# A windowed attention pipeline on one core: another order of its steps on four engines, and norms in pairs

## What is computed

```python
for i in range(DEPTH):                      # DEPTH 6, HEADS 16, DIM_HEAD 64, WINDOW 32
    x = attn_layer(shift_tokens(x), ...) + x
    x = ffn_layer(shift_tokens(x), ...) + x
...
q, k, v = split(x @ Wqkv)                   # per head
q = l2norm(q) * qs; k = l2norm(k) * ksc
q = q * cos * scale + rotate_half(q) * sin * scale
k = k * cos / scale + rotate_half(k) * sin / scale
# each window of 32 queries looks at its own 32 keys and the 32 before
sim  = einsum('bhwie,bhwje->bhwij', bq, bk2) * 8, masked
out  = einsum('bhwij,bhwje->bhwie', softmax(sim), bv2)
return concat_heads(out) @ Wo
```

## Time and profile before

| what | us |
|---|---|
| median of 3 runs | 2237.3 |
| lowest, highest | 2233.07, 2239.87 |
| the profiled execution | 2229.49 |
| its span, first to last instruction | 2227.6 |

### The profile page before, as it was taken

How to read it: one execution, slowest core, us unless ns; L and a number is a source line. 1 busy time by engine, 2 the same in 40 slices (tenths; PEclk the granted TensorE clock), 3 DMA queues, 4 the chain that set the end, 5 groups by cost and what they waited for, 6 DMA issues and landing times. The chain is left out here.

```text
span 2227.6 us, 82947 instructions
## 1 busy us (share of the span) xinstructions
PE 2062.4 (93%) x32996; PEld 1476.9 (66%) x32996; DVE 1627.3 (73%) x3071; ACT 1472.3 (66%) x4549; POOL 1238.2 (56%) x1377
## 2 busy tenths in 40 slices
PE   7788888999899999999998999999999989999997
PEld 3232335985776976876867859768768678587672
DVE  1598986985876966867857759668678577596673
ACT  4532326976775967867767759668678667596682
POOL 1465865764753754854647537548546465365450
PEclk9888989999999999999999999999999999999999
DMA  1321202111121211211111212112211111121010
GB/s 59 133 72 60 75 29 79 41 40 33 42 74 30 50 36 33 65 56 37 40 34 37 79 27 50 35 36 55 64 37 42 34 35 42 28 50 28 24 31 19
DMA packets 148094, 104.31 MB, mean 47 GB/s; under 512 B 15778, under 2 KB 140256, under 8 KB 146176
## 3 DMA queue, kind: packets, MB, share of 16 engines
q1 hardware_dynamic: 147712, 99.07, 16.0%
HBM read 48.31 MB, written 1.18 MB: 22 GB/s over the span
## 5 line engine op out<-in xcount | busy, mean ns | idle before, releaser
L1133 ACT ACTIVATE PR<-ps,MN 128x64 f32<-128x64 f32 x1536 | 356.6, 315 | 391.3 <-DVE MN L1255 391.1
L1383 POOL TENSOR_TENSOR QK<-PC,PS 128x256 f32<-128x256 f32 x384 | 278.9, 726 | 601.0 <-DVE PS L1294 584.1
L1388 POOL TENSOR_TENSOR QK<-QK,RN 128x512 f32<-128x512 f32 x384 | 401.6, 1046 | 158.0 <-ACT RN L1123 130.5
L1002 PE MATMUL ps<-W,XS 128*128 128x256 f32 x1536 | 396.5, 381 | 4.6 <-PEq L64 4.1
L973 PE MATMUL ps<-V,PT 64*32 64x65 f32 x12288 | 301.0, 219 | 1.2
L1002 PEld LDWEIGHTS ps<-W,XS 128*128 128x128 f32 x1536 | 262.7, 191 | 25.6 <-issue 4.9
L1384 POOL TENSOR_TENSOR QK<-PC,PS 128x256 f32<-128x256 f32 x384 | 279.1, 727 | 0.0
L988 PE MATMUL ps<-ident,QK 128*128 128x128 f32 x1536 | 252.0, 287 | 29.3 <-POOL QK L1388 29.3
L973 PEld LDWEIGHTS ps<-V,PT 64*32 64x32 f32 x12288 | 257.6, 105 | 11.3 <-ACT PT L1174 5.9
L1255 DVE TENSOR_REDUCE MN<-ps 128x4 f32<-128x256 f32 x384 | 161.6, 421 | 141.7 <-PE ps L953 135.7
L1278 DVE TENSOR_REDUCE SS<-SQ 128x8 f32<-128x512 f32 x384 | 259.3, 675 | 4.4 <-ACT SQ L1165 4.4
(11 more groups left out here) (138 smaller groups left out, 3439.5 us busy)
## 6 DMA issues: line engine op xcount, KB each, us to landing
V<-V SPq DMA_DIRECT2D x384, 97.5 KB, 2.3
scr<-B_rows SPq DMA_DIRECT2D x32, 512.0 KB, 3.5
V<-V SPq DMA_DIRECT2D x288, 32.5 KB, 2.2
W<-in_Wqkv SPq DMA_DIRECT2D x40, 192.0 KB, 2.8
TC<-in_tcos SPq DMA_DIRECT2D x6, 1024.0 KB, 5.3
TS<-in_tsin SPq DMA_DIRECT2D x6, 1024.0 KB, 8.5
WO<-in_Wo SPq DMA_DIRECT2D x6, 512.0 KB, 4.3
W<-in_W SPq DMA_DIRECT2D x6, 341.0 KB, 3.5
```

The costliest lines, as they stand in the source:

```text
L1002: mm = nc.tensor.matmul(ps[:, par, k * 2 * P:(k + 1) * 2 * P], cols[k], W[:, i, 0:2, :].rearrange("p t m -> p (t m)"), start=True, stop=True)
L1133: e = nc.scalar.activation(PR[:, m % 2, h, slot * DH:(slot + 1) * DH], ps[:, 4 + h, slot * DH:(slot + 1) * DH], ACT.Exp, scale=-1.0, bias= ...
L1383: nc.gpsimd.tensor_tensor(QK[:, par, :, 0:hd], PC[:, par, :, 0:hd], PS[:, par, :, hd:DH], ALU.add)
L1388: nc.gpsimd.tensor_tensor(QK[:, par, :, :], QK[:, par, :, :], bcast_last(RN[:, par, :], DH), ALU.mult).then_inc(qk, 1)
```

## The change

Seven things change, all in `transformer_block` but the joining of the tables:

- q's and k's transposes are called ahead of the scores, and their step is n-4 instead of n-3.
- The 16 scores and 16 values come in another order. Before, the scores ran through one head's windows, then the other's, and the values of both halves of rows went to bank 6 through four of the eight tiles. Now `spread_tiles` runs through all eight tiles in turn, in both, and the values of the two row halves go to banks 5 and 6. The scores and the transposed output move to banks 3 and 4, v's projection to bank 5, p to bank 6.
- Waits that were left to others are written out. The output's transposes, the masks and p's transposes wait for themselves.
- Log and root of the norms are taken for two steps at once on 16 columns, in odd rounds, in `norm_pair`; the clamp follows in even rounds as a `tensor_scalar` with a constant.
- ScalarE's order is new: q and k, norms, exponentials, squares, output, p, v. VectorE's order is new: the rotary products stand ahead of the sums of squares, and these are of step n, no longer n-1.
- GpSimd's rotation is of step n-2 instead of n-1.
- The tables lie in one tensor TCS, and one VectorE instruction of 1024 elements makes both products.

The diff, cut to its core:

```diff
+        spread_tiles = [(0, 0), (1, 2), (0, 1), (1, 3), (0, 2), (1, 0), (0, 3), (1, 1)]
...
             def out_transposed(n):
...
-                if n >= NSTEPS:
-                    wait(pe, pr, min(n - 5, NSTEPS))
-                    wait(pe, oT, m)
+                wait(pe, pr, min(n - 5, NSTEPS))
+                wait(pe, oT, m)
                 pe.wait_ge(on, m + 1)
...
-                for h in range(2):
-                    for j in range(8):
-                        slot, quad = slot_quad(j)
-                        c0 = PAD + s * STEP + j * WIN
-                        mm = nc.tensor.matmul(ps[32 * quad:32 * quad + 32, 4 + h, slot * DH:(slot + 1) * DH],
+                pe.wait_ge(qkT, m + 1)
+                for slot in range(2):
+                    for h, quad in spread_tiles:
+                        c0 = PAD + s * STEP + window(slot, quad) * WIN
+                        mm = nc.tensor.matmul(ps[32 * quad:32 * quad + 32, 3 + h, slot * DH:(slot + 1) * DH],
...
                 for h in range(2):
-                    for j in (0, 2, 1, 3, 4, 6, 5, 7):
-                        slot, quad = slot_quad(j)
+                    for slot, quad in spread_tiles:
+                        j = window(slot, quad)
...
-                        mm = nc.tensor.matmul(ps[32 * q:32 * q + 32, 6, g * (DH + 1):(g + 1) * (DH + 1)],
+                        mm = nc.tensor.matmul(ps[32 * quad:32 * quad + 32, 5 + slot, h * (DH + 1):(h + 1) * (DH + 1)],
...
                 wait(pe, v_cp, n)
+                wait(pe, on, n - 6)
                 for k in range(2):
-                    if k == 1:
-                        wait(pe, pr, n - 4)
...
+            def norm_pair(n):
+                p = (n - 3) // 2
+                if n % 2 == 0 or not 0 <= p < NSTEPS // 2:
+                    return
+                act.wait_ge(ssm, p + 1)
+                nc.scalar.activation(SS[:, p % 2, :], SS[:, p % 2, :], ACT.Ln, scale=LN_SCALE).then_inc(lns, 1)
+                act.wait_ge(lns, p + 1)
+                wait(act, qk, 2 * p - 2)
+                nc.scalar.activation(RN[:, p % 2, :], SS[:, p % 2, :], ACT.Exp, scale=-0.5, bias=lnb[:]).then_inc(rn, 1)
...
-                root(n)
+                copy_qk(n)
+                norm_pair(n)
                 exponents(n)
+                if u == U_FFN and t >= 0:
+                    load_set(nc, act, GELU)
+                squares(n)
                 copy_out(n)
-                if u == U_FFN and t >= 0:
-                    logs(n)
-                    load_set(nc, act, GELU)
-                copy_qk(n)
-                squares(n)
                 copy_p(n)
                 copy_v(n)
...
+                both = TCS[l % 2][:, :, 2 * s:2 * s + 2, :].rearrange("p t k c -> p t (k c)")
+                nc.vector.tensor_tensor(PCS[:, par, :, :, :].rearrange("p t a d -> p t (a d)"),
+                                        ps[:, par, :].unsqueeze(1).to_broadcast([P, 2, CH]), both, ALU.mult).then_inc(prods, 1)
...
                 least(n)
                 normalise(n)
+                tables(n)
                 norms(n)
-                tables(n)
+                clamp_pair(n)
```

More of the change, by code:

```diff
@@ L71, in mamba_block @@
         XT, XRES, XS, MOD, ident, ones, epsc = (keep[k] for k in ("XT", "XRES", "XS", "MOD", "ident", "ones", "epsc"))
-        W, QKS, QK4, TC, TS, MASKB, identb = (keep[k] for k in ("W", "QKS", "QK4", "TC", "TS", "MASKB", "identb"))
+        W, QKS, QK4, TCS, MASKB, identb = (keep[k] for k in ("W", "QKS", "QK4", "TCS", "MASKB", "identb"))
         ps = keep["ps"]
@@ L815, in transformer_block @@
         stored = [sem("stored%d" % c) for c in range(NCH)]
-        s_vz, s_ones, s_v0, s_lnb, s_least = (
-            sem(k) for k in ("s_vz", "s_ones", "s_v0", "s_lnb", "s_least"))
+        s_vz, s_ones, s_v0, s_lnb = (
+            sem(k) for k in ("s_vz", "s_ones", "s_v0", "s_lnb"))
         qkv_dram = d["Wqkv"].rearrange("l p (t i m) -> l p i t m", t=3, i=PAIRS)
@@ L913, in _, with window @@
             sp.wait_ge(w_2, 32 * DEPTH)
-        def slot_quad(j):
-            return (j % 4) // 2, (j // 4) * 2 + j % 2
+        def window(slot, quad):
+            return quad // 2 * 4 + slot * 2 + quad % 2
+        spread_tiles = [(0, 0), (1, 2), (0, 1), (1, 3), (0, 2), (1, 0), (0, 3), (1, 1)]
         @block.tensor
@@ L939, in scores @@
                     pe.wait_ge(s_ones, 2)
-                if n >= NSTEPS:
-                    wait(pe, pr, m)
-                    wait(pe, oT, m - 3)
+                wait(pe, pr, m)
+                wait(pe, oT, m - 3)
                 for h in range(2):
-                    if h == 0:
-                        wait(pe, qkT, min(n - 3, NSTEPS))
-                    if h == 1 and n >= 7:
-                        pe.wait_ge(v_sh[(n - 7) % 4], 32 * ((n - 7) // 4 + 1))
-                    nc.tensor.matmul(ps[:, 4 + h, 0:P], identb[:], MASKB[:, int(s == 0), h, :], start=True, stop=True)
-                for h in range(2):
-                    for j in range(8):
-                        slot, quad = slot_quad(j)
-                        c0 = PAD + s * STEP + j * WIN
-                        mm = nc.tensor.matmul(ps[32 * quad:32 * quad + 32, 4 + h, slot * DH:(slot + 1) * DH],
+                    nc.tensor.matmul(ps[:, 3 + h, 0:P], identb[:], MASKB[:, int(s == 0), h, :], start=True, stop=True)
+                pe.wait_ge(qkT, m + 1)
[3 more added lines that the diff above has]
+                        mm = nc.tensor.matmul(ps[32 * quad:32 * quad + 32, 3 + h, slot * DH:(slot + 1) * DH],
                                               QKT[DH * h:DH * h + DH, 0, c0:c0 + WIN],
@@ L978, in qk_transposed @@
             def qk_transposed(n):
-                m = n - 3
+                m = n - 4
                 if not 0 <= m < NSTEPS:
                     return
+                wait(pe, qkT, m)
                 pe.wait_ge(qk, m + 1)
-                if n < 5:
-                    wait(pe, qkT, m)
                 for x in range(2):
@@ L1005, in project @@
                 wait(pe, v_cp, n)
+                wait(pe, on, n - 6)
                 for k in range(2):
-                    if k == 1:
-                        wait(pe, pr, n - 4)
-                    mm = nc.tensor.matmul(ps[:, 3, k * P:(k + 1) * P], cols[k], W[:, i, 2, :], start=True, stop=True)
+                    mm = nc.tensor.matmul(ps[:, 5, (2 + k) * P:(3 + k) * P], cols[k], W[:, i, 2, :], start=True, stop=True)
                 mm.then_inc(v_ps, 1)
@@ L1015, in p_transposed @@
                     return
-                if n >= NSTEPS:
-                    pe.wait_ge(pr, m + 1)
-                    wait(pe, v_cp, NSTEPS)
-                if n < 8:
-                    wait(pe, pT, m)
+                wait(pe, pT, m)
+                wait(pe, on, m)
+                pe.wait_ge(pr, m + 1)
                 for h in range(2):
-                    if h == 1 and n < NSTEPS:
-                        wait(pe, oT, n - 7)
-                    mm = nc.tensor.transpose(ps[:, 3, (2 + h) * P:(3 + h) * P], PR[:, m % 2, h, :], ident[:])
+                    mm = nc.tensor.transpose(ps[:, 6, (2 + h) * P:(3 + h) * P], PR[:, m % 2, h, :], ident[:])
                 mm.then_inc(pT_ps, 1)
@@ L1181, in copy_v @@
                     act.wait_ge(s_ones, 2)
-                wait(act, pT_ps, n - 5)
                 wait(act, o_ps, n - 7)
@@ L1370, in scale_tables @@
                 pool.wait_ge(w_tab[l % 2], 32 * ((l + 1) // 2))
-                for tab in (TC, TS):
-                    piece = tab[l % 2][:, 2 * j:2 * j + 2, :]
+                for tab in range(2):
+                    piece = TCS[l % 2][:, tab, 2 * j:2 * j + 2, :]
                     nc.gpsimd.tensor_tensor(piece, piece, QK4[:].rearrange("p x h d -> p (x h d)").unsqueeze(1)
```

103 lines of the change are left out of this document (41 added, 62 removed).

## The result

| | before | after |
|---|---|---|
| median us (4 runs each) | 2235.72 | 2318.73 |
| lowest, highest | 2233.07, 2239.87 | 2314.26, 2320.05 |
| span of the profiled execution | 2227.6 | 2317.8 |

The changed kernel takes 1.0366 times as long, with a 95% interval of 1.0343 to 1.0389. The forecast was 2298 us, +2.7%, in a range of 2258 to 2370. The time went the way that was forecast and lies in the range; the loss was a third larger than forecast.

A forecast was written before the change was run, and what follows sets the result against it. TensorE's own stream bounds an ordinary step before, at 3.45 us; after, loops through the output's copy. +70 us for 235 ordinary steps and -9 for 11 phases' longer steps give +61: 2298 us, range 2258 to 2370.

The forecast's parts named there:

- The loop over the output's copy: ScalarE copies the output behind squares that wait for the projection; TensorE's next output transposes wait for it: +70 us.
- Loop A: From projection through squares, output's copy, transposes and tiles to the next projection: 3.72 us, 3.78 with a second restart.
- loop B: From the scores through minimum, exponentials, squares, output's copy and transposes to the next scores: 3.71 us.
- The size of an ordinary step: An ordinary step takes 3.75 us instead of 3.45, 0.30 more in each of 235 steps: +70 us.
- The tiles: Scores and values on TensorE over eight tiles, to the next full-width instruction: 0.79 us instead of 1.01, 0.22 less.
- the tiles gain nothing: Rival: scores and values keep their 10 and 17 ns a record; +125 us, 2362 us; chance 0.16.
- The first part of a phase: Steps u = 6 to 9, 11, 12: the wait is covered, shorter tiles count; about 1.1 us gained a phase.
- Rounds 13 and 14: Behind the second variance, q's and k's transposes wait for GpSimd's delayed rotation: 1.2 us longer for the two together.
- The feed-forward round: Step u = 15: first gelu 3.6 us after the projection instead of 4.48, 0.8 to 0.9 gained.
- Pairs, clamp, joined product at nothing: Paired norms, fewer clamps and one joined product lie on engines with slack in an ordinary step: costed at nothing.
- the copy is in time: Rival: output's copy ends before p's transposes, TensorE's stream sets 3.23 us; 2176 us; chance 0.09 including cancelled gains.
- the clock falls: Rival: TensorE idles, its clock halves; 2500 us and more; chance 0.03 together with a late pair of norms.

The follow-up runs named there:

- a1: The changed kernel with the output's copy moved ahead of the squares again on ScalarE: 2203.76 us, 0.9869 of the kernel before.
- b1: The kernel before with only the output's copy moved behind the squares on ScalarE: 2470.65 us, 1.1079 of the kernel before.
- a2: The changed kernel with the old tile orders of scores and values, the values' two banks kept: 2351.03 us, 1.0535 of the kernel before.
- a4: a1 with the second variance in round 13 instead of 12: 2168.79 us, 0.9715 of the kernel before.
- b2: The kernel before with the second variance in round 13 instead of 12: 2211.99 us, 0.9894 of the kernel before.
- a5: The changed kernel with the joined rotary product split into two instructions again: 2315.24 us, 1.0365 of the kernel before.
- a11: The changed kernel with the norms' clamp, log and root taken in every step instead of in pairs: 2310.06 us, 1.0347 of the kernel before.
- a9: a1 with the norms' clamp, log and root taken in every step instead of in pairs: 2236.89 us, 1.0014 of the kernel before.
- a6: The changed kernel with q's and k's transposes behind the values and ScalarE's old order, output's copy ahead of squares: 2226.9 us, 0.996 of the kernel before.

## The prediction against the traces

**The loop over the output's copy: right.** It was named as the term that decides, with its place and its pieces. Of them, in the order of the chain (predicted, then measured): projection to squares 1.07, 1.17; to the copy 0.49, 0.49; the copy with its hand-over to the matmul 0.39 + 0.06, 0.47; L929 to L979 0.22, 0.24; 0.44, 0.44; 0.20, 0.20; tiles 0.79, 0.82 in this step and 0.79 in the median one. Loop A binds: ScalarE is idle for 0.13 between the exponentials' last instruction, by the 0.81 of the earlier trace rows at about 1067.98, and the squares at 1068.10, so loop B was ready about that much earlier, near 3.7 as forecast. a1 and b1 are the direct test of the term.

**The size of an ordinary step: the term mis-sized.** Forecast 3.75, measured 3.81, in 234 steps 12 us too little. Two things make it. Loop A added up to 3.78 in the prediction's own working, and 3.75 was then taken, below the longer of two loops though the longer one sets the step. And the projection behind the values takes 1.13 instead of 1.03: the first full-width group behind tiles lasts 0.10 longer, and since the change moved the transposes of q and k away from that place, the projection pays for it, at the head of the loop. The prediction had given the change back 0.14 inside the tile block and 0.06 for a restart, but left the projection's length in the loop at 1.03. Against that the 0.06 for a restart, taken twice in 3.78, was too much: L929 to L979 grew by 0.02 behind the wait, and the 0.06 behind the values was no restart but the longer first group, here 0.10.

**The tiles: right in sum.** The block takes 0.79 in the median step, as forecast, and 1.01 before. Of its parts, the 10 and 17 ns of the kernel before were misread, since scores and values overlap in the earlier trace rows: by first and last records they are 9 and 19 ns, and the change back is 0.15 in all three kernels, forecast 0.14. The scores' records came down to 8 ns and the values' to 10, but a gap of 0.09 opened between the two, which the prediction had not. That the errors cancel to 0.79 is luck in part. The rival "the tiles gain nothing" would have been 2362 us; a2, which takes back only the orders, is at 2351, since it kept 0.09 of the block's gain.

**The first part of a phase.** Rounds 6 to 9, 11 and 12 gained 0.12 to 0.17 each, in sum 0.86, where 1.1 was forecast; round 10, which the prediction left out, lost 0.15. Rounds 13 and 14 lost 0.76 and 0.57, together 1.33 where 1.2 was forecast, and here the number is luck. 0.7 of it is the loop's 0.35 in each, which the prediction had left out of these rounds, and in the changed kernel's own trace no wait behind GpSimd stands in them: all 20 of its waits (18.0 us, before 27.7) are in the tables' rounds. What does stand there is the loop's own wait, in round 13 longer: the exponentials start 0.74 behind the projection (1029.63 to 1030.37) instead of 0.25, behind ScalarE's work for the variance, the copy of q and k, and the log and root of the pair, and L929 starts 2.50 behind it instead of 2.13. The mechanism that the prediction gave showed only where the loop was gone (a1, under a4 above). The feed-forward round gained 0.85, as forecast, and mostly by the mechanism named. Its timeline:

```profile
1037.86 1.13 PE L993 MATMUL ps<-W,XS 128*128 128x256 f32 x4
...
1039.08 1.28 ACT L54 ACT_TABLE_LOAD   x1
1040.37 0.60 ACT L1154 ACTIVATE SQ<-ps 128x512 f32<-128x512 f32 x1
...
1041.65 1.30 ACT L1196 ACTIVATE HID<-ps,VEC 128x512 f32<-128x512 f32 x2
```

First gelu 3.79 behind the projection, before 4.48, forecast 3.6. All together the longer rounds gave 1.9 us instead of 9, a miss of 7: the six rounds' 0.24, round 10's 0.15, rounds 13 and 14's 0.13, and 0.05 each for rounds 15 and 16, by 11.

**The ends: about 7 us in these two traces, and not clearly the change's.** "Start and end of the program are the same" was forecast. The first projection starts 2.7 later, but over all twelve traces, with the same mixer in each, it starts anywhere from 357.2 to 364.8. Behind the last projection the changed kernel takes 80.4 and the kernel before 76.6, the shortest of the twelve; b1 and b2, whose steps are spread over the rounds as before, take 80.0 and 81.1. So a longer end needs no new spread of the steps. In windows, columns as in the earlier trace rows, the changed kernel shows this:

```profile
2269.70:2276.50 6.80, 5.93 (x7) 2.29 (x8) 0.00 (x0) 1.32 (x2) 2.04 (x2) 0.50 0.00 0
```

The granted clock is at half, 1.2 GHz, for 6.8 us, after 28 us in which TensorE was busy 21 (2237 to 2265), and stretches like it, of 6.8 us or more together, are in every trace but that of the kernel before. It can account for at most 3.4 of the 3.75 us, an estimate; no run tests it.

The sum of the misses, 12 + 7 + 7 and 3 for the tables' steps, is 29: 61 forecast, 90 measured between the spans of the two profiled executions. Between the medians it is 83, and the miss 22, so some 7 of the 29 belong to the single executions.

**Pairs, clamp, joined product at nothing: right for this kernel, and only for it.** a5 shows it for the joined product and a11 for the pairs with their clamp. With the loop gone the pairs' saving is worth 33 us (a9 against a1). Work that is free while something else bounds is not free in the better version.

**The signs that were named.** Steps of 3.65 to 3.85: 3.81. Squares at 1.1: 1.17. Tile block under 0.8: 0.79. Idle in front of L929 of some 0.4 us: 0.46 by the matmuls' starts. The 100 us in all are 91.9 by the row, 115 by a1. The releaser was wrong: the row names "issue", and only the timeline (copy ends 1068.96, weights load 1069.03) and a1 show whose wait it was.

**The rival "the copy is in time"**, 2176 us, didn't come, but a1 tells what its stream is worth: 3.30 a step instead of its 3.23, and 2203.76 us. The rival "the clock falls" didn't come either: between 400 us and the last projection the granted clock is 1.00 in both kernels, in the changed one with TensorE idle 0.30 in 3.80 us by the window. Behind the last projection it did fall, as told above.

## What to carry to other kernels

In a pipeline written out by hand, look for a single-buffered region whose release is queued behind an instruction that waits for the current round: follow it from the producer round to the producer again and add up. If that sum exceeds the busiest engine's own stream, the sum sets the step, and the order of one line can cost more than all the savings beside it bring, as here. When a change mixes gains and one such loop, undo the one line first: here 115 us came back, and the gains that it had hidden were then worth measuring one by one.

## What the runs showed of the hardware

- **A tiny instruction on VectorE can last as long as GpSimd's running one.** In a9 the clamp of 128x8, from SBUF to SBUF, took 0.60 us beside GpSimd's 0.73 and ended with it (1093.35 and 1093.32); in the mean it took 0.487, and in pairs 0.217, with 0.16 where nothing ran beside it (1069.36 in the changed kernel). Over all of a9, 292 clamps began while GpSimd ran, and every one ended within 0.08 us of GpSimd's instruction; the 68 that met none took 0.17. The L1280 of the earlier trace rows, 0.42 in the mean for 8 columns, does the same: 0.56 in the median beside GpSimd, 0.17 without. The Trainium skill, page "SBUF — State Buffer", section "SBUF: two separate sides", says that VectorE and GpSimd share a port pair under an exclusive lock: a VectorE instruction in a two-port mode or with two SBUF inputs, or one of GpSimd, holds it for the whole instruction, and the other is blocked. The trace agrees.
- **Tiles of 64x32, 32 float32 records.** Eight tiles in turn instead of two or four: scores 8 ns a record instead of 9, values 10 instead of 19, the whole block 0.79 us instead of 1.01, as told under a2.
- **The first full-width group behind tiles lasts 0.06 to 0.10 longer.** The projection takes 1.13 us where it follows the values (the changed kernel, a1, a2, a9) and 1.03 where it follows transposes (before, b1, a6); four transposes take 0.66 behind the values (before, b1, a6) and 0.60 elsewhere.
- **"issue" in front of an instruction that waits for several things** can be a wait for another engine: 91.9 us in the changed kernel, 3.2 once the copy was ahead.
